# A three-round graph kernel on one core: edge loops written out, longer rings, node features reloaded, and a running maximum taken straight from gathered rows

## What is computed

```
x_src, x_dst = x[src], x[dst]
e   = relu((x_dst - x_src) @ theta_w.T + theta_b + x_src @ phi_w.T + phi_b)
x   = layernorm(x + segment_max(e, dst))                     # empty segments give 0
hv  = x @ W_in + b_in
for W, b in ((W_u0, b_u0), (W_u1, b_u1)):
    m  = relu(concat(hv[src], edge_attr) @ W + b)
    hv = hv + segment_max(m, dst)                            # where a node has in-edges
out = layernorm(x + relu(hv @ W_ro + b_ro))
```

## Time and profile before

| | before |
|---|---|
| median of 3 runs | 4077.67 us (4070.99 to 4083.26) |
| span of the profiled execution | 4130.5 us |
| PE busy | 2714.2 us, 66% |
| POOL busy | 2475.7 us, 60% |
| DVE busy | 1491.2 us, 36% |
| ACT busy | 179.9 us, 4% |
| DMA | 749.89 MB, mean 182 GB/s |

### The profile page before, as it was taken

How to read it: one execution, slowest core, us unless ns; L and a number is a source line. 1 busy time by engine, 2 the same in 40 slices (tenths; PEclk the granted TensorE clock), 3 DMA queues, 4 the chain that set the end, 5 groups by cost and what they waited for, 6 DMA issues and landing times.

```text
span 4130.5 us, 37131 instructions
## 1 busy us (share of the span) xinstructions
PE 2714.2 (66%) x5810; PEld 1143.5 (28%) x5810; DVE 1491.2 (36%) x3659; ACT 179.9 (4%) x555; POOL 2475.7 (60%) x2539
## 2 busy tenths in 40 slices
PE   6554554555555567777677677767677767676766
PEld 4221221222122433322233233243222222222224
DVE  2443443544344533333333333312323233333325
ACT  1000000000000210000000000020000000000003
POOL 3556555565555656665666656675566656666656
PEclk8667677776777788999888888889888888898878
DMA  6455555555555656666665566665566556565655
GB/s 210 159 169 170 171 166 163 184 179 170 163 173 175 156 180 197 199 196 197 198 198 193 192 196 201 193 125 177 185 195 201 187 189 198 187 208 183 199 164 115
DMA packets 330569, 749.89 MB, mean 182 GB/s; under 512 B 61299, under 2 KB 177117, under 8 KB 330558
## 3 DMA queue, kind: packets, MB, share of 16 engines
q0 software_dynamic: 136368, 334.92, 30.0%
q1 hardware_dynamic: 123630, 350.60, 22.6%
q10 hardware_dynamic: 70560, 64.26, 5.2%
HBM read 408.77 MB, written 340.77 MB: 181 GB/s over the span
## 4 chain that ended last, share of the span: by engine, by line
another core or an unknown queue 19%; issue 17%; PE 14%; POOL 9%; DVE 6%; DVEq 3%; DMA 3%; ACTq 1%; ACT 0%; POOLq 0%; SPq 0%
PE edge_ps L737 8%; PE edge_ps L735 6%; POOL hv_sb L576 5%; DVE hist L364 5%; POOL gath L550 4%; DMA gath<-table,idx_ring 2%; DVEq L364 1%; ACTq L607 1%; DVEq L361 1%; DVEq L360 1%; PE edge_ps L691 0%; PE side_ps L691 0%; DVE junk L297 0%; DVEq L446 0%
## 5 line engine op out<-in xcount | busy, mean ns | idle before, releaser
L550 POOL DMA_INDIRECT gath<-table,idx_ring x2352 | 2226.6, 947 | 1486.2 <-issue 758.1
L737 PE MATMUL edge_ps<-gath,ident 128*128 128x512 f32 x2352 | 1472.1, 722 | 577.1 <-issue 249.1
L364 DVE SCALAR_TENSOR_TENSOR hist<-hist,keep,edge_ps 128x256 f32<-128x256 f32 x1568 | 753.1, 480 | 1655.1 <-remote 702.3
L735 PE MATMUL edge_ps<-w_e,he_sb 128*128 128x512 f32 x1568 | 949.2, 691 | 517.3 <-DVE hist L364 474.9
L737 PEld LDWEIGHTS edge_ps<-gath,ident 128*128 128x128 f32 x2352 | 476.1, 223 | 1438.4 <-issue 750.6
L735 PEld LDWEIGHTS edge_ps<-w_e,he_sb 128*128 128x128 f32 x1568 | 320.2, 217 | 994.3 <-DVE hist L364 656.9
L364 DVE SCALAR_TENSOR_TENSOR hist<-hist,lift,edge_ps 128x256 f32<-128x256 f32 x784 | 376.4, 480 | 580.0 <-issue 424.0
L611 ACT COPY idx_ring<-src_sb 128x8 int32 x294 | 57.9, 197 | 3590.8 <-PE edge_ps L737 1252.2
L691 PE MATMUL side_ps<-w_theta,back_T 128*128 128x256 f32 x196 | 80.0, 549 | 149.2 <-issue 86.8
L576 POOL DMA_INDIRECT hv_sb<-runs,end_zero x98 | 151.2, 1542 | 32.7 <-issue 29.3
L759 PE MATMUL side_ps<-ident,gath 128*128 128x128 f32 x294 | 58.4, 332 | 96.0 <-ACT gath L621 42.6
(11 more groups left out here) (106 smaller groups left out, 798.2 us busy)
## 6 DMA issues: line engine op xcount, KB each, us to landing
runs<-hist SPq DMA_DIRECT2D x588, 512.0 KB
he_sb<-in_he ACTq DMA_DIRECT2D x392, 128.0 KB
gath<-table,idx_ring POOLq DMA_INDIRECT x2352
table<-hist SPq DMA_DIRECT2D x63, 256.0 KB
back_T<-in_xT ACTq DMA_DIRECT2D x49, 128.0 KB
x_sb<-in_x SPq DMA_DIRECT2D x49, 128.0 KB
x1T<-hist SPq DMA_DIRECT2D x7, 896.0 KB
back_T<-x1T ACTq DMA_DIRECT2D x49, 128.0 KB
```

What stands on the lines that cost most here:

```text
L364: V.scalar_tensor_tensor(hist[:, j, :], hist[:, (j - 1) % BODY, :], fresh[:, bass.ds(i * BODY + j, 1)], edge_ps[:, (j // 2) % BANKS, (j % ...
L550: pool.indirect_dma_start(gath[:, j, :], None, tables[r], bass.IndirectOffsetOnAxis(idx_ring[:, j:j + 1], 0)).then_inc(gathered[j // 2], 16)
L735: T.matmul(bank, he_sb[:, c, at:at + P], w_e[r - 1][:, :], start=True, stop=False)
L737: T.matmul(bank, ident[:, :], gath[:, 2 * q:2 * q + 2, :].rearrange("p s f -> p (s f)"), start=(r == 0), stop=True).then_inc(pair_summed, 1)
```

## The change

1. The loops over turns and groups are written out: every wait is for a constant, and no register is computed.
2. `gath` has 48 slots (`G`) and `hist` 40 (`H`). POOL waits once for every 2 steps, for the pair 48 steps back, and reads its indices from `src_sb` directly. `idx_ring` and the copies to it are gone.
3. In round 0 DVE takes the running maximum straight from `gath`; the PE product with the unit matrix is left out in this round.
4. SP writes `hist` out 8 steps at a time, and ACT loads edge features for 8 steps at a time into four buffers.
5. `x_sb` is gone. SP loads the features of each group into a ring of three buffers in `gath` ahead of each residual sum, and writes the normed ones to a new DRAM tensor `x1` to load them again at the end.
6. `back_T` has two buffers, and ACT, not DVE, copies the side product to `hv_sb`.
7. The first features (`xT`) are loaded a whole group at a time into four buffers. Several tiles that are only used in setup lie in `gath`, slots 32 to 47, so that the first gather waits until all of setup is done.

Cut to its core:

```diff
-CH = 4
-NCH = BODY // CH
-PAIRS = BODY // 2
+PAIRS = STEPS // 2
+G, H = 48, 40
+SC = 8
+HC = 8
+NHE = 4
...
-        x_sb = sb("x_sb", [P, TILES, D])
-        gath = sb("gath", [P, BODY, D])
-        hist = sb("hist", [P, BODY, D])
-        idx_ring = sb("idx_ring", [P, BODY], i32)
+        gath = sb("gath", [P, G, D])
+        hist = sb("hist", [P, H, D])
...
+            def edge_maxima(r):
+                fresh = lift if r == 0 else keep
+                for t in range(STEPS):
+                    s = r * STEPS + t
+                    if r == 0 and t % BODY == BODY // 2:
+                        pick_rows(t // BODY + 1, col_no[:, :])
+                    if s % SC == 0 and s >= H:
+                        dve.wait_ge(stored[s // SC % NS], 16 * (s // H))
+                    if s % 2 == 0 and r == 0:
+                        dve.wait_ge(gathered[s % G // 2], 2 * 16 * (s // G + 1))
+                    elif s % 2 == 0:
+                        dve.wait_ge(pair_summed, s // 2 - PAIRS + 1)
+                    if s > 0:
+                        dve.wait_ge(state_done, s)
+                    edges = gath[:, s % G, :] if r == 0 else edge_ps[:, (s // 2) % BANKS, (s % 2) * D:(s % 2 + 1) * D]
+                    V.scalar_tensor_tensor(hist[:, s % H, :], hist[:, (s - 1) % H, :], fresh[:, t:t + 1], edges,
+                                           ALU.add if r == 0 else ALU.mult, ALU.max).then_inc(state_done, 1)
...
+            def load_x(n, g):
+                if n == 0 and g == 0:
+                    sp.wait_ge(state_done, STEPS)
+                if n == 1 and g == 0:
+                    sp.wait_ge(pair_summed, (ROUNDS - 1) * PAIRS)
+                    sp.wait_ge(x1_kept, 16 * GROUPS)
+                if g >= X_BUFS:
+                    sp.wait_ge(norm_step, NORM_STEPS * (n * GROUPS + g - X_BUFS) + 2 * GT)
+                to = gath[:, X_AT + g % X_BUFS * GT:X_AT + (g % X_BUFS + 1) * GT, :]
...
+                sp.dma_start(to, of).then_inc(x_landed[g % X_BUFS], 16)
...
-            def gather_edges(r, i):
-                for c in range(NCH):
-                    if c % (NCH // 2) == 0:
-                        pool.wait_ge(idx_ready, (r * TURNS + i) * 2 + c // (NCH // 2) + 1)
-                    pool.wait_ge(pair_summed, (r * TURNS + i) * PAIRS + (c + 1) * CH // 2)
-                    pool.sem_inc(waits_met, 1)
-                    for j in range(c * CH, (c + 1) * CH):
-                        pool.indirect_dma_start(gath[:, j, :], None, tables[r],
-                                                bass.IndirectOffsetOnAxis(idx_ring[:, j:j + 1], 0)).then_inc(gathered[j // 2], 16)
+            def gather_edges(r):
+                for t in range(STEPS):
+                    s = r * STEPS + t
+                    if s % 2 == 0 and G <= s < STEPS + G:
+                        pool.wait_ge(state_done, s - G + 2)
+                    elif s % 2 == 0 and s >= G:
+                        pool.wait_ge(pair_summed, (s - G) // 2 - PAIRS + 1)
+                    pool.indirect_dma_start(gath[:, s % G, :], None, tables[r],
+                                            bass.IndirectOffsetOnAxis(src_sb[:, t:t + 1], 0)
+                                            ).then_inc(gathered[s % G // 2], 16)
...
+                if r == 0:
+                    pool.wait_ge(w_loaded, 16 * len(weight_loads))
+                    pool.wait_ge(setup_step, setup_at["all"])
+                    pool.wait_ge(none_written, 16)
...
+            def keep_back(r, i):
+                act.wait_ge(back_product, r * TILES + i + 1)
+                nc.scalar.copy(hv_sb[:, i, :], back_ps).then_inc(back_kept, 1)
```

More of the change, by code:

```diff
@@ L154, in gnn_kernel @@
         w_loaded = sem("w_loaded")
-        x_loaded = sem("x_loaded")
+        x_landed = [sem(f"x_landed{b}") for b in range(X_BUFS)]
         none_written = sem("none_written")
@@ L415, in conv_sums @@
             def conv_sums(g):
-                if not isinstance(g, int):
+                if g > 0:
                     dve.wait_ge(normed, g * GT)
+                dve.wait_ge(x_landed[g % X_BUFS], 16 * (g // X_BUFS + 1))
                 def summed(k):
                     dve.wait_ge(row_landed[k], 16 * (g + 1))
-                    return V.scalar_tensor_tensor(work[k], of_tile(hv_sb, g, k), 0.0, of_tile(x_sb, g, k), ALU.max, ALU.add)
+                    return V.scalar_tensor_tensor(work[k], hv_tile(g, k), 0.0, x_ring[g % X_BUFS][k], ALU.max, ALU.add)
                 layer_norm(0, g, work, summed)
@@ L427, in stage_with_bias @@
                 for k, end in tile_pairs:
-                    dve.wait_ge(product, 2 * TILES + g * GT + end + GT)
+                    dve.wait_ge(product, 2 * TILES + g * GT + end)
                     if k == 0:
@@ L494, in write_x1T, with write_out @@
                              hist[:, 0:GT, :].rearrange("p k f -> p (k f)")).then_inc(x1T_written, 16)
-            with sp.Fori(0, GROUPS) as g:
+            def write_out(g, k, end, rows):
+                sp.wait_ge(normed, (GROUPS + g) * GT + end)
+                sp.dma_start(a["out"][(g * GT + k) * P:(g * GT + end) * P, :].rearrange("(k p) f -> p k f", p=P)
+                             if rows == P else a["out"][NODES - rows:NODES, :],
+                             gath[:, GT + k:GT + end, :] if rows == P else normal[k][0:rows, :]).then_inc(staged_written, 16)
@@ L497, in _ @@
+            for g in range(GROUPS):
                 write_table(0, g)
@@ L589, in _ @@
         def _(act):
-            act.sem_inc(turned_out, GT)
-            act.sem_inc(product_out, GT)
             def stage(r, g):
                 for k, end in tile_pairs:
-                    act.wait_ge(product, r * TILES + g * GT + end + GT)
-                    if k == 0 and not (r == 0 and isinstance(g, int)):
+                    act.wait_ge(product, r * TILES + g * GT + end)
+                    if k == 0 and r * GROUPS + g > 0:
                         act.wait_ge(staged_written, WRITES * (r * GROUPS + g))
@@ L618, in copy_tile @@
             def copy_tile(r, g, k):
                 act.wait_ge(row_landed[k], 16 * (r * GROUPS + g + 1))
-                nc.scalar.copy(work[k], of_tile(hv_sb, g, k)).then_inc(tile_made, 1)
+                nc.scalar.copy(work[k], hv_tile(g, k)).then_inc(tile_made, 1)
             def turn_out(r, g, copy_next=False):
@@ L626, in turn_out @@
                     act.wait_ge(tile_turned, r * TILES + g * GT + end)
-                    act.wait_ge(product, (r + 1) * TILES + g * GT + end)
-                    if r == 0 and k == 0:
-                        act.wait_ge(x1T_written, 16 * (g + 1))
+                    if r * GROUPS + g > 0:
+                        act.wait_ge(product, (r + 1) * TILES + (g - 1) * GT + end)
+                    if r == 0 and k == 0 and g > 0:
+                        act.wait_ge(x1T_written, 16 * g)
                     nc.scalar.copy(hist[:, k:end, :].rearrange("p k f -> p (k f)"),
@@ L789, in _ @@
                 if r < 2:
-                    with pe.Fori(0, GROUPS) as g:
+                    for g in range(GROUPS):
                         turn(r, g)
@@ L795, in _ @@
                     turn(2, 0)
-                    with pe.Fori(0, GROUPS - 1) as g:
+                    for g in range(GROUPS - 1):
                         for k, end in tile_pairs:
```

407 lines of the change are left out of this document (197 added, 210 removed).

## The result

The changed kernel took 3894.99 us (median of 4 runs, 3887.66 to 3900.06), the kernel before 4077.76 us (4 runs, 4070.99 to 4083.26). The ratio is 0.9554, with a 95% interval of 0.9529 to 0.9578. The forecast was 3620 us: the direction is right and the time lies in the range of 3360 to 3900 us, but 183 us were gained where 458 were forecast.

The account below looks back on a forecast made before the run. POOL's gathers, 1.25 us apart, plus its pauses on full rings were taken as the bound. Setup 83, rounds 1029, 1092 and 1092, stretches 119.0, 110.6 and 124.9, extras 13: 3663.5 us, times 0.987, say 3620; range 3360 to 3900 us.

Parts of the forecast that it names:

- the forecast's own upper bound: Whole kernel: every round at 1.43 us a step, giving 3799 us.
- rounds 1 and 2 at 1.52 us a step: Rival: only round 0 gains, rounds 1 and 2 stay near 1202 us each; 3830 us, chance 0.15.
- The factor 0.987: Whole kernel: median time 4077.67 us over profiled span 4130.5 us, used to scale 3663.5 us to 3617.
- 10 us from the last gather to the join: End of each round: 10 us added after the last gather, against 13 us in round 1 before.
- POOL can run 48 steps ahead: Longer rings: POOL's lead grows from 16 steps to 48, or 20 us to 60, so 5 to 10 us delays don't stop it.
- Round 0 at 1.30 us a step: Round 0 without PE: 784 steps at 1.30 us plus 10 us, 1029 us.
- Rounds 1 and 2 at 1.38: Rounds 1 and 2 with longer rings: 784 steps at 1.38 us plus 10 us, 1092 us each.
- The formula behind the upper bound: Rounds 1 and 2: delay grows to 8.5 us behind 48 gathers, (48 x 1.25 + 8.5) / 48 = 1.43 us a step.
- Between and at the end: Stretches between and behind rounds stay 119.0, 110.6 and 124.9 us; feature reloads and last stores add 13 us.
- floor: Rival: delays wholly absorbed, POOL streams without pause in all rounds; 3376 us, chance 0.25.
- Gathers held up by DVE: Rival: in round 0 DVE steps with two SBUF inputs lengthen gathers, up to 376 us; 3950 us, chance 0.06.
- Starving: Rival: without full pauses of POOL, consumers in rounds 1 and 2 fall to 2.03 us a step; 4620 us, chance 0.06.

Follow-up runs that it names:

- set 1: First set of follow-up runs, on chip 5 in condition A; the kernel before took 4073.70 us there.
- e1: Changed kernel with POOL at most 16 steps ahead instead of 48; 3817.71 us, ratio 0.9364, in condition A.
- e2: Changed kernel with a memset of one byte per partition on POOL behind each gather; 3868.57 us in condition A.
- e12: Changed kernel with lead of 16 steps, later wait for setup, round 0 through PE again and stores of 4 steps; 3859.47 us, ratio 0.9428, in condition A.
- condition B: Chip state, lasting a whole set of runs, in which the unchanged kernel before took 3398 to 3406 us.
- e9: Changed kernel, unaltered, run again in condition B; 3441.63 us, ratio 1.0108 to the kernel before.
- e13: Changed kernel with PE and DVE working on only one step in eight; 3785.89 us in condition A.
- condition A: Chip state, lasting a whole set of runs, in which the unchanged kernel before took 4074 to 4101 us.
- set 2: Second set of follow-up runs, on chip 5 in condition B; the kernel before took 3402.22 us there.

## Why the prediction was right and wrong

The sum was 3663.5 us of span, times 0.987. Measured are 3890.5 us of span. The forecast gain of 458 us was two and a half times what came, and the steps that failed are two: that a round ends 10 us after its last gather, and that round 0 goes at 1.30 us a step because PE is out of it. That the time lies in the range of 3360 to 3900 us is luck: it is beyond the forecast's own upper bound (3799 us, which its own numbers put at about 3795), and the room above that bound was made for another case, rounds 1 and 2 at 1.52 us a step. The 275 us between 3620 and 3895 are these:

- **The factor 0.987: 48 us.** It was the median of the timed runs over the span of another execution, the profiled one. The runs of before in set 1 have time and span of the same execution: 4067.84 and 4065.8 us, a ratio of 1.0005. So 0.987 is the difference between two executions, not between a time and its span, and should not have been carried over.
- **"10 us from the last gather to the join": 95 us.** The drains were 40.1, 42.8 and 42.0 us. The step "POOL can run 48 steps ahead" was followed up to the last gather and not to the last step: who is 41 to 45 steps ahead there leaves as many to be done. e1 shows it: with a lead of 16 the drains are 10.5 to 17.2 us at the same pace.
- **Round 0 at 1.30 us a step: 83 us.** It ran at 1.408. The reason given, that the late word from PE can't come into play, doesn't give 1.30: in e2 DVE is 3 steps behind and POOL is held up all the same with slots free, and e12 puts PE's share at some 26 us or less. What holds POOL up there is not known.
- **Rounds 1 and 2 at 1.38: 47 us.** They ran at 1.413 and 1.410, within the bounds of 1.25 and 1.43. The formula behind the upper bound is wrong all the same: it has a delay that a longer ring spreads over more steps, and e1 has the same pace with a lead of 16 as the change with 48. That 1.41 lies inside the bounds is luck too.
- **Setup: 7 us.** 90.1 instead of 83: the instruction that ended it (3.14 us) came later by 6.4 us.
- **Between and at the end: 6.8, -1.4 and 2.3 us** against 13 forecast with the last stores. The larger reload at the first stretch was underrated by 4 us.

The rivals: "floor" is what condition B shows, 1.25 us a step (1.26 in round 0 of e9), and there the kernel before has it too. "Gathers held up by DVE" was rightly small: 12 ns a gather in B. In A it is 977 against 949 ns (round 0 of e12), but these 28 ns are not DVE's for certain, since round 0 of e13, where DVE takes one step in eight, has 985 ns. The Trainium skill (SBUF — State Buffer, "Who interferes with whom") has the later instruction wait entirely; here the price was 10 us in B, not 376. "Starving" did not come.

The deeper failure is the reading of what bounds the kernel. The rows were read rightly, words late while POOL streams and in time when it stops, and the text said that it did not know what was shared. It then took the delay as a property of the kernel. In condition B the same instructions have no such delay, so some 670 us of the 4074 come from outside what the kernel's text settles. In A the change takes off 183 us net; in B it adds 35.

**What stays open.** What makes condition A. It isn't the chip, since chips 5 and 10 had both. Whether it is other work on the chip wasn't tried. The traces do tell the two apart by more than the delays: in A most updates of semaphores have no record. Of the 12544 that the landings of a round's gathers should make (16 for each gather), round 1 of the changed kernel has 2106 in A and 12497 in B, and the kernel before 1452 and 12509. Whether several updates arrive as one in A, or only their records are lost, or the recording itself takes part in the delay, no run here settles. It also means that the releasers that a trace of condition A names are less sure than the times at which its instructions start. Open is also why the pace in A is 1.37 to 1.45 us in every written-out version, though lead, gather bytes and the consumers' work were all varied. And so is which part of the change brought it down from 1.53 in rounds 1 and 2: the finer waits, the index copies, the loops' instructions, or the edge features loaded in larger pieces. The lead did not (e1), and stores of 4 steps kept 1.42 to 1.43 us there (e12).

## What to carry to other kernels

A ring's lead is paid back at its end where the consumers are slower than the producer can be (42.8 us in A, 14.1 us in B, for the same ring): try a smaller lead before a larger one, since here the deeper one only lengthened the drain. Before a stall is explained from one trace, see whether the same kernel has it in every set of runs; and judge a change that hides a stall also where the stall is absent, since there only its costs are left. And before a sum is scaled by the ratio of a timed run to a profiled span, see that both are of one execution.

## What the runs showed of the hardware

- The same program took 4074 us in set 1 and 3402 us in set 2 on chip 5, steadily within a set (4065.86 to 4084.08 and 3397.43 to 3404.64 over seven runs each), and 4101 and 3400 us on chip 10.
- In one stop in condition A a signal of PE reached three other engines 17.4 us after the end of its product, all three within 0.3 us of each other, and 8.6 us after POOL's last gather had ended. In round 1 of the changed kernel 244 of PE's 329 recorded signals stand over 0.2 us behind the end of their product in condition A, and none of 389 in condition B.
- In condition A the traces hold 1452 of the 12544 semaphore updates by the landings of one round's gathers, in condition B 12509 (kernel before, round 1).
- A gather of 64 rows holds POOL for 906 ns, one of 128 rows for 950 (condition B). Rows of 512 bytes instead of 1024 leave both POOL's 956 ns and the pace of 1.41 us as they were (condition A).
- A memset of 0.12 us between two gathers is free: it fits into the 0.30 us that POOL leaves between them.
